# A wide attention stage: the order of VectorE, ScalarE and TensorE at its opening and at its end

## The reference

```
# L1 attention: 32 query heads, 8 key/value heads, head size 128
q = x @ Wq.T; k = x @ Wk.T; v = x @ Wv.T          # per batch
q, k = rope(q), rope(k)                           # x*cos + rotate_half(x)*sin
scores = q @ k.T / sqrt(128), causal
out = softmax(scores) @ v                         # four query heads share one k, v
x = layernorm(x + out @ Wo.T)
```

## Time and profile before

| | |
|---|---|
| time, median of 3 runs | 2006.45 us (2006.06 to 2009.45) |
| profiled execution, its own time | 2006.38 us |
| span of its profile | 2004.7 us |
| mean granted TensorE clock | 0.979 of full speed |
| TensorE busy | 95% |
| VectorE, ScalarE, GpSimd busy | 57%, 43%, 43% |
| the wide attention, from the barrier before it to the one behind it | 315.1 to 1139.4 us |

### The profile page before, as it was taken

One profiled execution on the slowest core, in us unless ns is written; L12 is line 12 of the kernel. 1 busy time (PEld: TensorE's weight loads), 2 busy tenths in 40 slices (PEclk: granted clock), 3 DMA queues, 4 the chain that ended last, 5 costly groups with the idle time before them and its releaser, 6 DMA issues.

```text
span 2004.7 us, 29837 instructions
## 1 busy us (share of the span) xinstructions
PE 1894.5 (95%) x11008; PEld 1288.1 (64%) x11008; DVE 1140.3 (57%) x2177; ACT 858.7 (43%) x1896; POOL 868.8 (43%) x1380
## 2 busy tenths in 40 slices
PE   6999988999999999999999799999999998999998
PEld 3544446888888888888887687864444454544455
DVE  5676466666666666666666424235556355566465
ACT  1565544444444444444444333323555402565441
POOL 2454325545454545454544344323344312443352
PEclk9999988999999999999999899999999989999999
DMA  6113000101010101010100234203223003111101
GB/s 215 40 34 110 1 11 1 54 1 53 1 53 1 54 1 53 1 53 1 53 1 32 80 104 152 80 7 90 57 57 107 33 1 80 34 34 44 51 10 43
DMA packets 46211, 94.61 MB, mean 47 GB/s; under 512 B 7689, under 2 KB 35721, under 8 KB 43145
## 3 DMA queue, kind: packets, MB, share of 16 engines
q1 hardware_dynamic: 43474, 90.34, 13.7%
q10 hardware_dynamic: 2592, 2.36, 0.5%
HBM read 61.68 MB, written 2.10 MB: 32 GB/s over the span
## 4 chain that ended last, share of the span: by engine, by line
PE 78%; DVE 11%; ACT 5%; issue 3%; POOL 1%; DMA 1%; PEld 0%; SPq 0%; PEldq 0%; POOLq 0%; ACTq 0%; DVEq 0%
PE PS L1540 9%; PE PS L1440 9%; PE PS L463 6%; PE PS L566 6%; PE PS L1962 5%; PE PS L544 5%; PE PS L510 5%; PE PS L591 4%; PE PS L1518 4%; PE PS L1975 3%; PE PS L1469 3%; PE PS L1502 3%; PE PS L478 2%; PE PS L1933 2%; PE PS L512 2%
## 5 line engine op out<-in xcount | busy, mean ns | idle before, releaser
L990 ACT ACTIVATE PB<-PS 128x512 f32<-128x512 f32 x480 | 280.9, 599 | 236.5 <-PE PS L544 233.5
L897 POOL TENSOR_SCALAR_AFFINE_SELECT PB<-PB 128x256 f32<-128x256 f32 (+1 forms) x480 | 173.3, 365 | 320.2 <-ACT PB L990 313.9
L769 DVE TENSOR_REDUCE NM<-PS 128x2 f32<-128x1024 f32 x192 | 209.2, 1092 | 168.5 <-PE PS L512 167.2
L510 PE MATMUL PS<-KQ 96*128 96x512 bf16 (+3 forms) x768 | 185.3, 306 | 17.4 <-DVE NM L769 10.9
L544 PE MATMUL PS<-KQ 99*128 99x512 bf16 (+3 forms) x768 | 183.2, 304 | 4.8 <-ACT PB L990 3.4
L1856 POOL TENSOR_SCALAR PR<-PR,RCP 128x512 f32<-128x512 f32 (+3 forms) x256 | 134.3, 533 | 105.2 <-DVE RCP L1651 105.0
L1664 DVE TENSOR_REDUCE NX<-PS 128x1 f32<-128x512 f32 (+3 forms) x256 | 125.0, 488 | 79.9 <-PE PS L1491 74.0
L463 PE MATMUL PS<-XTT,WA 128*128 128x512 f32 x288 | 145.3, 611 | 13.5 <-DVE ident_masks_b L2597 12.0
L1726 ACT CAST OTH<-PS 128x512 fp32r<-128x512 f32 x64 | 37.6, 587 | 279.3 <-PE PS L1523 279.3
L1790 ACT ACTIVATE PR<-PS,NX 128x512 f32<-128x512 f32 (+3 forms) x256 | 137.2, 536 | 29.8 <-DVE NX L1664 25.8
L512 PE MATMUL PS<-ident_masks_b 128*128 128x128 bf16 x768 | 149.2, 223 | 0.0
(11 more groups left out here) (331 smaller groups left out, 4617.9 us busy)
## 6 DMA issues: line engine op xcount, KB each, us to landing
KQ<-HI SPq DMA_DIRECT2D x90, 128.0 KB, 2.4
KQ<-MID SPq DMA_DIRECT2D x72, 128.0 KB, 2.4
WB<-f_w SPq DMA_DIRECT2D x12, 768.0 KB, 4.3
WB<-w1o SPq DMA_DIRECT2D x8, 1024.0 KB, 7.9
WC<-f_w SPq DMA_DIRECT2D x10, 768.0 KB, 4.4
WB<-w1a SPq DMA_DIRECT2D x8, 768.0 KB, 4.4
WB<-w1b SPq DMA_DIRECT2D x8, 768.0 KB, 5.9
WA<-w SPq DMA_DIRECT2D x6, 1024.0 KB, 6.3
```

What stands on the lines that cost most here:

```text
L510: pe.matmul(ps, KQ[0:SR, self.query(G, h), i * P:(i + 1) * P], KQ[0:SR, self.key(G, h), 0:n], start=True, stop=False)
L769: x = dve.tensor_reduce(nm[:, h:h + 2, i], PS[:, b:b + 2, 0:(i + 1) * P], AX.X, ALU.max, negate=True)
L897: pool.affine_select(blocks, blocks, [[0, count], [1, P]], ALU.is_ge, 0.0, base=0, channel_multiplier=-1).then_inc(s16["probs_ready"].sem, 1)
L990: act.activation(PB[:, n % PBS, :], PS[:, 4 + n % 2, :], ACT.Exp, scale=self.scale)\
```

## The change

In the tail of `Ffn0`, `begin_low(0)` is moved ahead of the last turn, and `begin_high(1)` behind it; VectorE does `rope(0)` there, at the end of its work. In the wide attention VectorE does `rope(2)` ahead of head 0 and no longer between its maxima; ScalarE rounds it (`rope_high(2)`) ahead of head 0's first exponential; GpSimd forms its low part ahead of head 0's normalizations instead of behind them. At the end VectorE does `take_o(62)` and the four `low_pT` of head 63 ahead of `finish(2)` and `finish(3)` of tail 0; TensorE does `weighted(63)` ahead of the turns of tiles 2 and 3, and ScalarE `high_o(63)` ahead of the copies of those turns. No instruction is added or taken away but for one wait for the table.

```diff
@@ Ffn0.tensor
-                    if n in (8, 9):
-                        a1.begin_high(pe, n - 8)
+                    if n == 8:
+                        a1.begin_high(pe, 0)
+                    if n == 9:
+                        a1.begin_low(pe, 0)
                     if n >= 2:
                         b, t = divmod(n - 2, NT)
...
                         self.tails[b].turn(pe, t, self.x_bank(b, t))
-                for p in (0, 1):
-                    a1.begin_low(pe, p)
+                a1.begin_high(pe, 1)
+                a1.begin_low(pe, 1)
@@ Ffn0.vector
                 dve.wait_ge(self.tails[1].s_x.sem, self.tails[1].s_x.at(NT))
+                dve.wait_ge(s1_tab.sem, 16)
+                a1.rope(dve, 0)
@@ Attention1.tensor
                 for i in range(NT):
                     self.transpose_probs(pe, n, i)
+                self.weighted(pe, n)
                 for t in range(2, NT):
                     pe.wait_ge(self.tails[0].s_t.sem, self.tails[0].s_t.at(t - 1))
                     self.tails[0].turn(pe, t, PS[:, t % 2, :])
-                self.weighted(pe, n)
@@ Attention1.vector
-                dve.wait_ge(s1_tab.sem, 16)
-                self.rope(dve, 0)
                 self.rope(dve, 1)
                 self.rope_low(dve, 0)
                 self.take_v(dve, 0)
                 self.rope_low(dve, 1)
+                self.rope(dve, 2)
                 for n in range(GQ * NU):
...
-                        if n == 0 and i == 1:
-                            self.rope(dve, 2)
...
                 last = self.tails[0]
-                last.finish(dve, 2)
-                last.finish(dve, 3)
                 self.take_o(dve, GQ * NU - 2)
                 for i in range(NT):
                     self.low_pT(dve, GQ * NU - 1, i)
+                last.finish(dve, 2)
+                last.finish(dve, 3)
                 self.take_o(dve, GQ * NU - 1)
@@ Attention1.scalar
-                for p in range(2):
+                for p in range(3):
                     self.rope_high(act, p)
...
-                        if n == 0 and i == 2:
-                            self.rope_high(act, 2)
...
                 for i in range(NT):
                     self.copy_pT(act, GQ * NU - 1, i)
+                self.high_o(act, GQ * NU - 1)
                 for t in range(2, NT):
                     self.tails[0].take(act, t, PS[:, t % 2, :])
-                self.high_o(act, GQ * NU - 1)
@@ Attention1.gpsimd
                 for p in range(3):
                     self.sum(pool, p)
+                self.rope_low(pool, 2)
                 for n in range(GQ * NU):
...
-                    if n == 0:
-                        self.rope_low(pool, 2)
```

## The result

The changed kernel takes 1993.28 us (median of 4 runs, 1992.61 to 1994.72) against 2006.26 us before (2006.00 to 2009.45); the ratio is 0.9932 with a 95% interval of 0.9916 to 0.9947. On the prediction's base of 2006.4 that is 1992.8, a little under the low end of its range, 1993.0; 1995.7 was forecast. On that base the two comparisons give a gain of 13.6 and of 11.4 us where 10.7 was forecast. The 2.2 us between the two comparisons of one and the same pair of kernels cannot be the change's.

The account below looks back on a forecast made before the run. TensorE, busy 95% of the span, was taken as the bound, so only its waits could be shortened: 2006.4 - 5.5 (opening) - 6.0 (end) + 0.8 (clock) = 1995.7 us. Range 1993.0 to 2001.0.

Parts of the forecast that it names:

- the prediction's base: Time before the change that the sum started from: 2006.4 us (profiled execution 2006.38, median 2006.45).
- the first term: Opening, up to head 2's scores: they start at 339.9 instead of 345.4 us, a gain of 5.5 us.
- the second: End of the stage: the output's 48 matmuls start at 1112.95 instead of 1118.96 us, a gain of 6.0 us.
- the 0.8: End of the stage: allowance of 0.8 us for TensorE's clock falling; full half-rate cost put at 3.4 us.
- the price of the order: Feed-forward tail: TensorE stalls for the fourth part of XLa and ends 0.4 us later.
- (a): End: the clock falls because transposes do not hold it up; end gains 2.6 us, whole 1998.3. Chance 0.2.
- (c): End: finish blocks take_o in place of low_pT; gain there 2.7 us, whole 1999.0. Chance 0.04.
- (d): Opening: the low clock does not lift after the first scores; +22.4 us, so 2018. Chance 0.02.
- part 3: Opening, rotation 2 before the softmax: head 1's scores 4.1 us earlier, TensorE sets head 2's scores, gain 5.5 us.
- rival (b): Opening: GpSimd's queue delays the XLb parts, only 1.7 us of the first scores remains; whole 1999.5. Chance 0.12.
- my own upper bound of 6.0: Opening: the gain is at most 6.0 us without any half-rate stretch.
- the two bounds: Gains of 3.8 to 6.0 us in the opening and 2.6 to 6.3 at the end: 1994.1 to 2000.0.

Follow-up runs that it names:

- the two comparisons: The same changed kernel measured twice against the kernel before: ratio 0.9932 the first time, 0.9943 the second.
- e7: The kernel before with only TensorE's new order in the feed-forward's tail, rotation 0 left in the wide attention: ratio 1.0011.
- e6: The kernel before in its old order at the end, with GpSimd's split of the next weights held back until tail 0 is finished: ratio 0.9977.
- e1: The kernel before with the opening's edits alone (feed-forward tail, rotation 0 there, rotation 2 ahead of head 0): ratio 0.9965.
- e10: The changed kernel with eight unread matmuls more behind project 2, keeping TensorE busy ahead of the first scores: 1992.05 us, ratio 0.9934 to the kernel before.
- e2: The kernel before with the end's edits alone: ratio 0.9968.
- e8: The changed kernel with SyncE asking for the next stage's scales ahead of two weight blocks: 1990.79 us, ratio 0.9916 to the kernel before.
- e11: The changed kernel run again unaltered: 1994.33 us, ratio 0.9943 to the kernel before.
- e12: The changed kernel with both the scales asked for first and eight unread matmuls more behind project 2: 1987.97 us, ratio 0.9920 to the kernel before.
- e4: The kernel before with rotation 2 alone moved ahead of head 0, feed-forward tail left alone: ratio 0.9990.
- e3: The kernel before with the feed-forward's tail reordered and rotation 0 in it, rotation 2 left where it was: ratio 0.9987.
- e9: The kernel before with the feed-forward's tail reordered, rotation 0 in it, and eight unread matmuls more behind project 2: ratio 0.9987.

## Why the prediction was off

**What failed, in short.** Of the sum 5.5 + 6.0 - 0.8, the first term was too small (6.2 measured, because head 1 was priced too slow), the second nearly right (5.8), and the 0.8 for a falling clock at the end was 0. That is 12.0 us in place of 10.7. The rest of the first comparison's 13.6 lies outside the changed code, for which the sum had no term.

**Right.** The stage's start: 0.4 us was forecast as the price of the order; it is 7.19 - 6.77 = 0.4 in the changed kernel and 0.33 in e7. The first scores: 5.4 forecast, 5.35 behind the start. Head 1: 7.1 forecast behind head 0, 7.03. The end: 6.0 forecast, 5.8; low_pT was not held, the finishes were, and e6 shows the hold itself. Rivals (a), (c) and (d) are not in the trace.

**Mis-sized, and the wrong engine at the end of it: head 1 in part 3.** I had TensorE wait 0.65 us twice for exponentials and the weighted sum start 19.7 us behind the stage's start. It waited 0.38 us once (row at 330.37), and the weighted sum started at 332.91 - 313.92 = 19.0. I had GpSimd's qL done 0.5 us ahead of TensorE and wrote that TensorE sets head 2's scores. It was the other way round by 0.1 us: qL was forecast 23.9 us behind the start and ended 23.6 behind it, and TensorE was held for it. So rival (b)'s path is the one that bounds, though it took nothing back. The opening gives 6.2, not 5.5, and that is above my own upper bound of 6.0, which was the price without any half clock; e1 had no half clock there and e10 none either, and both took the same time as the changed kernel with it.

**Wrong: "I take 0.8"** for the clock at the end. It was 0: the clock is 1.00 in all stretches from 1099.5 on in the changed kernel, and in the same stretches of e2, e8, e10, e11 and e12, with the same 28.3 us from T to X. The Trainium skill (TensorE: Matmul & The Clock Gate, "Part 4: PE-mode transpose") says that a transpose does not count as busy for the clock in the same way as a matmul; by that, rival (a) was to come. Six traces have this end, with 0.71 us of work, transposes alone, in 2.3 us, and none shows a fall. They do not show that transposes count either.

**Missing: the rest of the program moves by itself.** The sum was made against one profiled execution, as if its other 1900 us were fixed. The same code ahead of H ended anywhere from 302.9 to 308.6 us in the profiled runs. This goes with the clock: the mean granted clock ahead of H is 0.98 in the two traces with H at 302.9 and 303.0, 0.97 in the seven with 305.1 to 307.0, and 0.96 in the five with 307.7 to 308.6. Behind X the same code took 864.1 to 868.8 us; there the clock does not explain it (0.98 both in e4, with 868.0, and in the changed kernel, with 866.0), and the cause stays open. The unchanged kernel's own runs in the later comparisons went from 2000.8 to 2012.2 us. With 6.2 and 5.8 the sum is 2006.4 - 12.0 = 1994.4; the first comparison's profiled run has 1.6 us of luck ahead of H and loses 0.7 behind X. The range should have had some 2 us on either side for this. Its low end, 1993.0, was 1.1 us under the 1994.1 that the two bounds gave, with no reason stated.

## What to carry to other kernels

When work is moved between two waits, ask which wait the half clock of TensorE will now lie on: a gain on one engine can be eaten by slower matmuls that another engine has begun to wait for (the traces of e3 and e9). When two queues are forecast to meet within 0.5 us, look in the trace which of them came last, the row of the weight load included. A VectorE operation from SBUF to SBUF should stand where nobody waits for it while GpSimd has a long instruction (e6: 3.2 us from one). Compare stretches between fixed points of the program and not spans, when the rest of the program moves the span by as much as the change does.

## What was not expected of the hardware

The granted clock falls and returns at places that differ from run to run of the same code, and this moves a stretch that holds a hole in TensorE's work: T to X with the old code took 34.11 us before, 34.10 in e3, 34.14 in e7, 34.79 in e4, 35.07 in e9 and 35.14 in e1. With the new orders the same stretches are free of it: H to head 2 was 30.80 to 30.84 us in all six traces with the new opening, T to X 28.29 to 28.31 in all six with the new end. In the opening the half clock came behind the hole of 2.0 us in the changed kernel, e8 and e11, and did not in e1; where it came it was hidden. At the end TensorE's longest idle time between T and the last unit's output is now 1.14 us, and the half clock came in none of the six traces.
